# Attention's q, k and v as three rounded products in the place of the retention's high weights

## What is computed

```
def _L0_attn_b_ref(x, wq, bq, wk, bk, wv, bv, wo, bo, rel_bias):
    ...
    def proj(w, b):
        y = jnp.einsum('blc,dc->bld', x, w) + b
        return y.reshape(Bx, Lx, HEADS, HEAD_DIM).transpose(0, 2, 1, 3)
    q = proj(wq, bq)
    k = proj(wk, bk)
    v = proj(wv, bv)
    scores = jnp.einsum('bhqd,bhkd->bhqk', q, k) / np.sqrt(HEAD_DIM)
    ...
    attn = jax.nn.softmax(scores + bias[None], axis=-1)
    out = jnp.einsum('bhqk,bhkd->bhqd', attn, v)
    ...
x = x + _L0_attn_a_ref(_layernorm(x, axis=-1), ...)
x = x + _L0_ffn_ref(_layernorm(x, axis=-1), ...)
x = x + _L0_attn_b_ref(_layernorm(x, axis=-1), ...)
x = x + _L0_ffn_ref(_layernorm(x, axis=-1), ...)
```

## Time and profile before

| | |
|---|---|
| median of 3 runs | 2796.4 us |
| the profiled execution's own time | 2794.24 us |
| its span | 2792.4 us |
| TensorE / VectorE / ScalarE / GpSimd busy | 96% / 77% / 62% / 45% |
| mean granted TensorE clock | 0.984 |

### The profile page before, as it was taken

How to read it: one execution, slowest core, us unless ns; L and a number is a source line. 1 busy time by engine, 2 the same in 40 slices (tenths; PEclk the granted TensorE clock), 3 DMA queues, 4 the chain that set the end, 5 groups by cost and what they waited for, 6 DMA issues and landing times.

```text
span 2792.4 us, 53679 instructions
## 1 busy us (share of the span) xinstructions
PE 2683.2 (96%) x19682; PEld 1468.2 (53%) x19682; DVE 2141.0 (77%) x4443; ACT 1741.2 (62%) x3671; POOL 1255.0 (45%) x1764
## 2 busy tenths in 40 slices
PE   7989999999999999999999999999999999999998
PEld 5733376433764338643486334854358533575334
DVE  6679756997669966699667995679956799468993
ACT  4438854588545884458744687537864478643885
POOL 3415544355433554335543455434553355533453
PEclk9979999999999999999999999999999999999999
DMA  7160001600015000250003400033000330013200
GB/s 195 31 136 2 24 9 39 144 17 24 9 49 134 17 31 2 61 122 17 32 1 77 105 17 32 1 93 89 17 32 23 92 69 17 31 31 99 54 2 16
DMA packets 71429, 139.18 MB, mean 50 GB/s; under 512 B 12784, under 2 KB 49696, under 8 KB 70016
## 3 DMA queue, kind: packets, MB, share of 16 engines
q1 hardware_dynamic: 69152, 135.29, 19.4%
q10 hardware_dynamic: 2016, 0.45, 0.1%
HBM read 86.02 MB, written 38.82 MB: 45 GB/s over the span
## 4 chain that ended last, share of the span: by engine, by line
PE 70%; DVE 16%; POOL 4%; issue 4%; ACT 2%; SPq 2%; DMA 2%; POOLq 0%; DVEq 0%; ACTq 0%
PE psum L882 18%; PE psum L941 16%; DVE mx L1821 8%; PE psum L655 7%; PE psum L1008 3%; PE psum L659 3%; PE psum L916 3%; PE psum L1064 2%; PE psum L977 2%; PE psum L715 2%; PE psum L842 2%; DVE nrm L1637 2%; POOL X L1938 1%; PE psum L1049 1%; DMA SQ<-mrow 1%
## 5 line engine op out<-in xcount | busy, mean ns | idle before, releaser
L1821 DVE TENSOR_REDUCE mx<-psum 128x1 f32<-128x512 f32 x2048 | 1264.9, 684 | 60.3 <-PE psum L882 59.6
L1470 ACT ACTIVATE Z<-psum 128x512 f32<-128x512 f32 x2048 | 1109.5, 598 | 277.1 <-PE psum L916 249.2
L2030 POOL TENSOR_TENSOR Z<-Z,W_low 128x256 f32<-128x256 f32 (+1 forms) x1152 | 713.3, 642 | 665.7 <-ACT Z L1470 658.5
L882 PE MATMUL psum<-SK,SQ 63*128 63x512 f32 x2048 | 760.5, 473 | 31.1 <-DVE mx L1821 26.2
L916 PE MATMUL psum<-SQ,SK 64*128 64x512 f32 x2048 | 755.9, 469 | 11.4 <-DMA SQ<-mrow 10.9
L941 PE MATMUL psum<-Z,Vx 128*17 128x256 f32 x8192 | 641.8, 388 | 0.4 <-POOL Z L2030 0.4
L882 PEld LDWEIGHTS psum<-SK,SQ 63*128 63x128 f32 x2048 | 309.2, 189 | 479.2 <-DVE mx L1821 362.1
L916 PEld LDWEIGHTS psum<-SQ,SK 64*128 64x128 f32 x2048 | 309.4, 188 | 84.0 <-ACT Z L1470 37.1
L941 PEld LDWEIGHTS psum<-Z,Vx 128*17 128x17 f32 x8192 | 138.2, 95 | 334.1 <-issue 274.3
L1938 POOL TENSOR_TENSOR X<-X,mixed 128x512 f32<-128x512 f32 x64 | 80.5, 1268 | 249.5 <-DVE mixed L1658 249.5
L1975 POOL TENSOR_TENSOR Z<-Z 128x512 f32<-128x512 f32 x64 | 82.0, 1281 | 243.1 <-DVE Z L1692 243.1
(11 more groups left out here) (135 smaller groups left out, 3517.1 us busy)
## 6 DMA issues: line engine op xcount, KB each, us to landing
W_low<-bias_rows SPq DMA_DIRECT2D x8, 2048.0 KB, 8.7
parts<-Z SPq DMA_DIRECT2D x32, 512.0 KB
W_low<-low_parts SPq DMA_DIRECT2D x7, 1536.0 KB, 6.7
X<-L_attn_a_x SPq DMA_DIRECT2D x8, 1024.0 KB, 5.5
SQ<-parts SPq DMA_DIRECT2D x32, 256.0 KB, 7.9
SK<-parts SPq DMA_DIRECT2D x32, 256.0 KB, 10.6
SQ<-parts SPq DMA_DIRECT2D x16, 512.0 KB, 6.5
SK<-parts SPq DMA_DIRECT2D x16, 512.0 KB, 14.3
```

The source lines that it names most:

```text
L882: pe.matmul(row_bank(c), SQ[rows_of(h, MAX_ROW), h // 2, i * P:i * P + P], SK[rows_of(h, MAX_ROW), h // 2, 512 * k:512 * k + 512], start=T ...
L1470: nc.scalar.activation(ring[:, n % RING, :], col_bank(n), ACT.Exp)\
L1821: nc.vector.tensor_reduce(mx2[:, blk % 2, col, k:k + 1], row_bank(c), AX_X, ALU.max)\
L2030: nc.gpsimd.tensor_tensor(ring[:, n % RING, a:z], ring[:, n % RING, a:z], band_exp[:, 4 * hg + cols_of(s)[i], at:at + z - a], ALU.mult)\
```

## The change

q, k and v are computed as three rounded products as the retention's are: (high n, high w), (high n, low w), (low n, high w). For that

- `nT` is written rounded by ScalarE for halves 2 and 3 of the norms; VectorE writes the rest of it (`ln_lows`, two subtractions of 512 columns a half, read from the transposes' bank) into columns 1536 to 3583 of `W_high`;
- the low parts of wq, wk and wv are made once, on ScalarE and VectorE in the first sequence's retention, kept in memory, and loaded into columns 0 to 1535 of `W_high` in each sequence (`qkv_load`, when the gates are done); `W_high` is loaded back whole at the fifth block of the maxima (`high_load`, 2 MB);
- items of q and k take three banks in turn, so item n waits for the low part of item n-3;
- v pair 1 stands in front of the transposes of the second half, no longer behind them; v pair 3 stands right behind pair 2, and the first mix product behind both, in front of the first rows.

```diff
-        QK_BANK = (3, 7)
+        QK_BANK = (3, 7, 6)
...
+            def qkv_load(b):
+                need(sp, p_g, b, NT)
+                sp.dma_start(W_high_words[:, 0:QKV_WORDS], qkv_scratch).then_inc(qkv_in.sem, 16)
...
+            def high_load(b):
+                need(sp, p_qkT, b, 8)
+                need(sp, p_vx, b, 4)
+                sp.dma_start(W_high_words[:, :], high_scratch).then_inc(high_in.sem, 16)
...
+                    if blk == 4 and b + 1 < B:
+                        high_load(b)
...
                 v_project(b, 2)
-                some_rows(1)
+                v_project(b, 3)
                 if b > 0:
                     mix_k(b - 1, 2, 0)
-                    some_rows(1)
-                v_project(b, 3)
+                    some_rows(2)
                 some_rows(1)
...
-                need(pe, c_lo, b, n - 1)
-                for c in range(C):
-                    mm = pe.matmul(bank[QK_BANK[n % 2]], WT[:, A_Q + side, c, h * P:h * P + P],
-                                   nT[:, c, 1 + 512 * g:513 + 512 * g], start=c == 0, stop=c == C - 1)
+                need(pe, c_lo, b, n - 2)
...
+                for i, j in ((0, 0), (0, 1), (1, 0)):
+                    if i == 1 and n in (0, 2):
+                        need(pe, n_low, b, n + 2)
+                    for c in range(C):
+                        mm = pe.matmul(bank[QK_BANK[n % 3]], qkv_parts[j][:, side, c, h * P:h * P + P],
+                                       n_parts[i][:, c, 512 * g:512 * g + 512],
+                                       start=i + j + c == 0, stop=i == 1 and c == C - 1)
...
                     if n == 2:
                         v_project(b, 0)
+                        v_project(b, 1)
                         ln_transposes(b, 3)
-                        v_project(b, 1)
                         pe.wait_ge(fn_T, 2 * norm_at(b, 3) + 2)
...
+            def qkv_high():
+
+                act.wait_ge(s_wts, 7)
+                nc.scalar.copy(qkv_staged[0], WT[:, A_Q:A_V + 1].rearrange("p w c n -> p (w c n)")).then_inc(s_qkv_high, 1)
...
+            def ln_lows(b, n):
+
+                g = n % 2
+                need(dve, qkv_in, b, 1)
+                need(dve, p_w, b, NT)
+                for c in range(C):
+                    dve.wait_ge(fn_T, 2 * norm_at(b, n) + c + 1)
+                    tok = slice(512 * g, 512 * g + 512)
+                    nc.vector.tensor_tensor(n_parts[1][:, c, tok], ln_bank(b, n, c), n_parts[0][:, c, tok],
+                                            ALU.subtract).then_inc(n_low.sem, 1)
...
+                ln_lows(b, 2)
                 ln_stats(b, 3)
-
                 ln_norms(b, 3)
                 if b > 0:
                     ln_stats(b - 1, 4)
 
                 for n in range(8):
+                    if n == 2:
+                        ln_lows(b, 3)
                     if n == 4 and b > 0:
                         ln_norms(b - 1, 4)
```

71 lines of the change are left out of this document (59 added, 12 removed).

## The result

| | before | after |
|---|---|---|
| median of 4 runs each, same chip | 2796.86 us (2796.13 to 2798.44) | 2810.41 us (2810.07 to 2811.57) |
| ratio, 95% interval | | 1.0049 (1.0035 to 1.0063) |
| the profiled execution's own time | 2794.24 us | 2810.23 us |
| its span | 2792.4 us | 2808.4 us |
| mean granted TensorE clock | 0.984 | 0.981 |

The account below looks back on a forecast made before the run. VectorE, not the 96% busy TensorE, was taken to bound half of every sequence. Late first maxima +8.1, first sequence -1 and clock falls +5.4 gave +12.5 us on the 2796.4 median: 2808.9 us, range 2782 to 2830.

Parts of the forecast that it names:

- The stage, step by step: Eighth sequence, item 0 to the transposes among the rows: TensorE waits 1.0 and 1.5 us at item 2, first maximum 1.16 later.
- The window of 181.2 us: Sequence 7's score rows and attention loop up to the last maximum: VectorE works 174.47 us and is the bound.
- The prices: Cost of new work: q or k item 1.38 us, v pair 1.45, VectorE's subtractions 0.685 each, 0.61 apart.
- +8.1 for seven sequences: First maximum of each sequence behind the first: about 1.2 us lost in each, +8.1 us in all.
- The first sequence, -1: First sequence, with no older half: transfers leaving earlier give -2 us, new set-up steps +1, together -1.
- the set-up steps: First sequence: two copies on ScalarE and one subtraction on VectorE of 1536 columns, +1 us (0 to 3).
- The maxima's transfers: First sequence: transfers that start from item low parts leave some 1.5 to 2.8 us earlier, -2 us (0 to -4).
- The clock, +5.4: At item 2: a second 6.8 us fall to half clock in two of seven sequences, +2.7 us each.
- the wait at 2536.0: Second transposes waiting for VectorE's norms until 2536.6; absorbs 0.7 of the 3.4 us that a clock fall costs.
- Rival 1: TensorE's saved time comes through, rows no later: about 2782 us, 2761 at most; decided by first row before 2543.9; chance 0.2.
- Rival 4: Clock falls at item 2 in every sequence and again where TensorE waits at 2553: 2818 to 2838 us; chance 0.2.
- theory A: First of the rival expectations written for each follow-up run, with its own mechanism and time each; not part of the prediction.

Follow-up runs that it names:

- e6: e5 plus VectorE's statistics of the other last half before the first half's mixes, its norms right behind the first pair of maxima; 2796.18 us, ratio 1.0001.
- e5: e3 plus GpSimd's four additions of the output bias put behind the squares of the third mixing; 2795.92 us, ratio 1.0002.
- e1: Changed kernel with the old order of the mixed rows, v pair 3 behind the first rows and mix product; 2807.93 us, ratio 1.0041.
- e4: Changed kernel without high-weight reloads and with low weights loaded only in the first sequence, so later results are wrong; 2811.61 us, ratio 1.0054.
- e8: Changed kernel with only v pair 1 and its copy put back behind the second half's transposes; 2810.15 us, ratio 1.0051.
- e3: Changed kernel with the old row order and VectorE's second pair of subtractions before the low parts of items 0 and 1; 2797.14 us, ratio 1.0002.
- e9: e5 with the last v pair put ahead of the first row, into TensorE's wait for transfers; 2812.31 us, ratio 1.0056.
- e10: e6 with the last v pair put ahead of the first row; 2802.88 us, ratio 1.0024.
- e11: e6 with eight of the third v pair's twelve products made twice from the second sequence on, output unchanged; 2795.22 us, ratio 0.9996.
- e7: Changed kernel with item 2's first four products made twice from the second sequence on, ahead of its wait, output unchanged; 2807.34 us, ratio 1.0039.

## Why the prediction was right, and where it was not

The mechanism came as forecast, and the time within 1.5 us. So close a hit is in part luck: the profiles differ by 16.0 us where the sum had 12.5, and the terms behind the first missed in both directions.

**The stage, step by step**, counted from item 0 in an undisturbed sequence. Transposes at 5.66 forecast, 5.73 measured. Item 2 at 7.5, measured 7.54 (the wait was 0.78, not 1.0, behind transposes that took 1.03 of their own). The subtractions let TensorE go at 10.0, measured 10.11; wait 1.5 forecast, 1.37 measured. The transposes of the sequence before, at item 6, at 15.3, measured 15.27. First row at 23.75, measured 23.75. First maximum 24.2, measured 24.28, against 23.09: 1.19 later where 1.16 was forecast. The second norms of the sequence before 29.6, measured 29.65; transposes among the rows 31.8, measured 31.80. Here one thing was not told: that these transposes would *wait* 1.23 us, in place of 0.18. TensorE reaches them with v pair 3 no longer between the rows. Taking such a wait away brought nothing (e6 against e5), but it is one of the three places at which the clock falls.

The window of 181.2 us in which VectorE was found to be the bound runs 2.4 us past the last maximum; up to that it is 172.13 of 178.82 us, the same 96%.

**The prices.** Items 1.38 forecast and 1.40 to 1.44 measured, v pairs 1.45 and 1.42, subtractions 0.61 apart and 0.60 (2535.52 and two in 1.29 us).

**+8.1 for seven sequences**: +8.1 by the undisturbed maxima. That the order makes it, and not the added products or transfers, is shown by e1 to e4: with the old order of the rows alone the undisturbed first maximum is back at 23.1, with both orders undone it stood at 22.85, and without the loads nothing changed.

**The first sequence, -1**: -0.65 in all, of other parts. Its item 0 starts 0.10 later where 1 was put for the set-up steps; in the experiments' profiles it starts 0.4 to 2.7 us later, so one pair of profiles does not fix this term. The low clock of this sequence lasts 41.0 us in place of 34.1; what that costs is not separated. The maxima's transfers, forecast 1.5 to 2.8 earlier, left about 1; from item 0 to the score behind them it is 57.8 us, before 58.7.

```profile
188.55 0.79 PE L963 MATMUL psum<-SQ,SK 64*128 64x512 f32 x1 [7.68 <-DMA SQ<-mrow]
```

**The clock, +5.4**: the term that was mis-sized, though it came out near enough. Forecast were two falls of 6.8 us, at item 2, +2.7 each (by its own times 0.6 us, not 0.7, goes into the wait at 2536.0, which makes it 2.8). The trace has five of 3.4 us: two at item 2 (+1.3 and +1.1 to the first maximum), two at the wait among the rows, not forecast (+1.7 each), one at the wait for a block's maxima (+3.5 with the wait). Together about 9 us in this profile, against which the four other sequences stand with -1.2 behind the first maximum. That the falls come at waits is read from all profiles; that the time hangs on them is not: e8 with one and e4 with two take as long, with more waits for the maxima, a term that the prediction did not have behind the first sequence. The length was taken from the fall at the end of the mixed rows, which still lasts 6.8 here; that a fall may last half of this was in no row.

**Rivals.** Rival 1 decided by the first row before 2543.9 on its clock; it stood at 2545.05. Rival 4 wanted a fall at item 2 in every sequence and at the transposes among the rows; it came in two at either place.

**My expectations for the experiments** were worse than the prediction. e1, e3, e5, e6, e9, e10 and e11 each came out 3 to 19 us above the time given for theory A. In e3 and e9 the reason is GpSimd beside VectorE's norms. The step that failed in e5, e6 and e11 is the same: that a microsecond won at the first maximum comes through whole in every sequence. e5's three undisturbed sequences won 1.3 us there against before, and at their last maximum 0.7, 0.9 and 1.2 were left; in e11's six sequences without an extra fall it was 0.4 in the mean of 1.3. The changed kernel's two undisturbed sequences lost 1.2 us at the first maximum, and their last maxima came 0.8 and 1.3 us later (202.99 for 202.24, 203.66 for 202.41). What stands in the way behind is, by the rows, the second block's way through the transfers: 0.9 us of waits in sequences 2 to 8 before, 4.7 in e5, 7.8 in e11, 18.8 in e10. No run takes this way out, so that it is the next bound is read, not tested, and e6, with 2.7, kept no more in total than e5 with 4.7. Why it shows in one sequence and not in its neighbour stays open, as for the falls.

## What to carry to other kernels

Ask when the bound engine can start its next piece, and not how busy the other one is: TensorE was 96% busy and lost work, and the kernel became slower: the time won on the products went into waits for their new parts, and the new order put more work in front of the rows for which VectorE, the bound behind them, had to wait. Before a step is moved on VectorE, look at what GpSimd does in its new place, and before a piece of TensorE's work is moved away, look at the wait it covered. In this kernel a wait of a microsecond or two on TensorE stood, now and then, beside a fall of its clock.

## What the runs showed of the hardware

- VectorE's norms (four, 256 columns, from X to nrm) took 1.37 us with GpSimd idle, 2.10 beside one or two of its squares, 2.42 beside its additions, and 3.99 beside both without a gap; GpSimd's additions took 5.0 to 5.1 us with or without them. The maxima, which read PSUM, took 1.28 the pair in either case. The Trainium skill, "SBUF — State Buffer", section "Who interferes with whom", has VectorE and GpSimd share a pair of SBUF ports; a tensor_scalar on VectorE, which the norms are, can take both ports and then contends with GpSimd, the one that issues first holding the pair for its whole instruction, and a tensor_reduce never contends on this chip. That the norms grow longer and the maxima don't agrees with it; that GpSimd's additions keep their time beside the norms does not show the lock from the other side.
- The granted clock fell from 1.0 to 0.5 for 3.4 us as well as for 6.8 and 10.2. Nearly all extra falls in sequences 2 to 8 began in, or within 2 us of the end of, an idle stretch of TensorE of 1.2 us or more: in none to four of seven sequences with the same stretch of 1.0 to 1.4 us, and in six where it was 3.0 to 3.1 us (e9). Where the stretch was filled to 0.2 to 0.5 us (e7 at item 2; e11 at the first row, with 0.9 us in one sequence) none came there in seven, but none came in e8 and e3 with stretches of 1.0 to 1.2 us either. Since each kernel has one profile, and e1 had four at item 2 where the changed kernel had two, the counts say that the places are right and neither how often nor that the idle stretch is the cause.
- SyncE takes 0.6 us to issue one transfer, so the twelve in front of the first row take 7.5 us, and the first row starts 2.4 us behind the start of the last issue (e6); in some sequences one of them takes 1.1 to 2.0 us.
